# Block-compressed attention, window attention and a routed feed-forward in one kernel: narrower compressed scores, the mask as a VectorE addition, compression in two strips, and new orders of the work

## The reference

```
kb = k[:, :nb * CS].reshape(b, nb, CB, -1) + pe[None, None]
vb = v[:, :nb * CS].reshape(b, nb, CB, -1) + pe[None, None]
ck = jnp.einsum('bnkd,k->bnd', kb, wk_comp)
cv = jnp.einsum('bnkd,k->bnd', vb, wv_comp)
sc = jnp.einsum('bhsd,bhnd->bhsn', q4, ck4) * SCALE
comp_mask = (jnp.arange(nb) + 1) * CS <= jnp.arange(s)[:, None]
a_comp = _masked_softmax(sc, comp_mask[None, None])
out_comp = jnp.einsum('bhsn,bhnd->bhsd', a_comp, cv4)
imp = sc.mean(axis=(1, 2))
_, top_idx = jax.lax.top_k(imp, TOPK)
```

## Time and profile before

| | |
|---|---|
| median of 3 runs | 2564.87 us |
| the profiled execution | 2562.29 us |
| its span, first to last instruction | 2560.4 us |
| mean granted TensorE clock | 0.96 of full |
| busy: TensorE, VectorE, ScalarE, GpSimd | 88, 68, 57, 35% |
| instructions | 55188 |
| DMA | 90.10 MB, mean 35 GB/s |

### The profile page before, as it was taken

How to read it: one execution, slowest core, us unless ns; L and a number is a source line. 1 busy time by engine, 2 the same in 40 slices (tenths; PEclk the granted TensorE clock), 3 DMA queues, 4 the chain that set the end, 5 groups by cost and what they waited for, 6 DMA issues and landing times.

```text
span 2560.4 us, 55188 instructions
## 1 busy us (share of the span) xinstructions
PE 2241.7 (88%) x18184; PEld 1447.0 (57%) x18184; DVE 1747.1 (68%) x4612; ACT 1446.9 (57%) x4829; POOL 889.9 (35%) x780
## 2 busy tenths in 40 slices
PE   3888999899998999989998999989999899977676
PEld 0756666556664666556664666646665566644443
DVE  3466777578776777667786677757777578765654
ACT  1245666556654666556664566646665466645553
POOL 0435333333334333243332433343332433333221
PEclk9998999999998999989999999989999899998888
DMA  6010001100011000110002000110001100020000
GB/s 213 21 34 14 26 26 34 55 26 22 26 43 47 18 26 26 41 48 26 26 22 68 22 26 18 51 39 26 26 26 38 51 26 22 22 66 17 13 18 13
DMA packets 48844, 90.10 MB, mean 35 GB/s; under 512 B 6760, under 2 KB 6760, under 8 KB 48544
## 3 DMA queue, kind: packets, MB, share of 16 engines
q1 hardware_dynamic: 39328, 69.51, 8.9%
q10 hardware_dynamic: 9216, 16.78, 1.8%
HBM read 69.45 MB, written 16.83 MB: 34 GB/s over the span
## 4 chain that ended last, share of the span: by engine, by line
issue 56%; POOL 28%; PE 8%; ACT 3%; DVE 3%; DMA 1%; POOLq 1%; SPq 0%; DVEq 0%; ACTq 0%
POOL csp L1211 6%; POOL css L1203 4%; POOL xc L1238 3%; POOL h_lo L1231 3%; POOL ra L1243 3%; POOL kr L1195 3%; POOL ra L1195 3%; POOL wo_s L1219 1%; ACT pw L982 1%; PE ps_m L690 1%; POOL wbt_s L1225 1%; PE ps_o L622 1%; PE ps_m L495 1%; PE ps_m L497 1%; PE ps_m L496 1%
## 5 line engine op out<-in xcount | busy, mean ns | idle before, releaser
L982 ACT ACTIVATE pw<-ps_s,wmax 128x128 f32<-128x128 f32 x1024 | 358.6, 378 | 147.3 <-DVE wmax L1455 147.3
L495 PE MATMUL ps_m<-w_hi,h_hi 128*128 128x512 f32 x768 | 352.8, 459 | 75.6 <-DVE rbf L1422 31.5
L992 ACT ACTIVATE pw<-pw,wden 128x128 f32<-128x128 f32 x1024 | 313.2, 388 | 124.3 <-DVE wden L1465 124.3
L1015 ACT ACTIVATE pT<-ps_s 128x512 f32<-128x512 f32 x240 | 142.4, 593 | 306.2 <-PE ps_s L616 222.7
L497 PE MATMUL ps_m<-w_hi,h_lo 128*128 128x512 f32 x768 | 308.3, 401 | 0.0
L496 PE MATMUL ps_m<-w_lo,h_hi 128*128 128x512 f32 x768 | 307.7, 401 | 0.0
L690 PE MATMUL ps_m<-wbt_s,h2T 128*128 128x512 f32 x512 | 259.7, 613 | 0.4 <-ACT zs L998 0.4
L655 PE MATMUL ps_m<-wo_s,aT 128*128 128x512 f32 x512 | 252.5, 616 | 0.9 <-ACT aT L1019 0.8
L1231 POOL TENSOR_TENSOR h_lo<-hT,h_hi 128x512 fp32r<-128x512 f32 x57 | 72.2, 1267 | 514.1 <-ACT h_hi L933 514.1
L495 PEld LDWEIGHTS ps_m<-w_hi,h_hi 128*128 128x128 f32 x768 | 147.7, 192 | 176.6 <-issue 90.1
L1211 POOL TENSOR_TENSOR csp<-csp,cden 128x256 f32<-128x256 f32 (+1 forms) x128 | 169.7, 1345 | 221.4 <-DVE cden L1504 221.4
(11 more groups left out here) (189 smaller groups left out, 4614.0 us busy)
## 6 DMA issues: line engine op xcount, KB each, us to landing
xa<-x_in SPq DMA_DIRECT2D x65, 256.0 KB, 2.7
xc<-x_in SPq DMA_DIRECT2D x64, 256.0 KB, 2.7
out<-t ACTq DMA_DIRECT2D x64, 256.0 KB, 2.0
wo_s<-wo_in SPq DMA_DIRECT2D x8, 1024.0 KB, 6.1
wbt_s<-wbt_in SPq DMA_DIRECT2D x8, 1024.0 KB
gbc<-gate_rows SPq DMA_DIRECT2D x24, 256.0 KB, 5.2
pw<-wmod_in SPq DMA_DIRECT2D x3, 1024.0 KB, 5.6
pT<-wmod_in SPq DMA_DIRECT2D x3, 1024.0 KB, 5.2
```

Source lines behind the costliest of these rows:

```text
L495: pe_.matmul(ps[:], h_hi[:, c, :], w_hi[:, col, c, :], start=(c == 0), stop=False)
L982: ins = act.activation(pw[:, hw, :], ps_w[:, j, i, 1, :], ACT.Exp, bias=wmax[:, hw:hw + 1], accum_out=wden[:, 0, hw:hw + 1])
L992: act.activation(pw[:, hw, :], pw[:, hw, :], ACT.Copy, scale=wden[:, 2, hw:hw + 1]).then_inc(wn_ok, 1)
```

## The change

- The compression scores go only over the 16 selected columns and the first 8 (t + 1) blocks: `cs_scores`, `cs_max`, `cs_subtract`, `cs_exps`, `cs_factor`, `cs_normalise` have 16 + 8 (t + 1) columns, that is 24 to 80. `transpose_cs`, `probs_copy` and `cs_values` take 72 to 128 rows.
- The four mask products are gone. `csmask` is float32, and VectorE adds it while it evacuates the scores (`cs_mask`), in place of ScalarE's `cs_copy`.
- `compress` writes two strips of 32 partitions: strip k takes tiles 4k to 4k + 3. `pe` is padded with zeros to 128 rows, so that all its products have 128 rows.
- The end part has functions of its own (`end_first`, `end_slot`, `last`) with orders of their own.
- The orders of `first_slot`, `slot` and `turn` are new on all four engines, and so are the banks.
- `gather` waits for the copy of the last V; the prologue's `split_h` waits for Q, K and V of the tile before. Part A, the loads and their order on SP's queue, the stores, and the prologue's `head` are otherwise as before.

The diff, cut to its core (for TensorE and VectorE the new order of a slot; `a` and `c2` conditions left out):

```
+def blocks_seen(t):
+    return (t + 1) * (P // CB)
...
-        csmask = sb("csmask", [P, NT, CS], BF16)
+        csmask = sb("csmask", [P, NT, CS])
...
-        parts = ((0, NSEL), (NSEL, CS))
+        def parts(t):
+            return (0, NSEL), (NSEL, NSEL + blocks_seen(t))
...
             def compress(seg, b, ba, tiles):
-                dst = ps_cv[NB:P, :]
+                half, per = NT // 2, NB // 2
+                strip = [ps_cv[NB + per * k:NB + per * (k + 1), :] for k in range(2)]
...
+                    for k in range(2):
+                        pe_.matmul(strip[k], pew[:, 0:per], pe_s[:, :], start=True, stop=False, skip_group_check=True)
...
+                    for k in range(2):
+                        mm = pe_.matmul(strip[k], blkw[:, off:off + per], v_s[:, half * k + t, :], start=False,
+                                        stop=(t == half - 1), skip_group_check=True)
...
             def cs_scores(b, t):
-                for j in range(4):
-                    pe_.matmul(ps_s[:, j, 0:4 * CS].rearrange("p (c n) -> p c n", c=4), ident_b[:, :],
-                               csmask[:, t, :].unsqueeze(1).broadcast_to([P, 4, CS]),
-                               start=True, stop=False, skip_group_check=True)
+                n = NSEL + blocks_seen(t)
                 for c in range(NC):
                     for j in range(4):
-                        mm = pe_.matmul(ps_s[:, j, c * CS:(c + 1) * CS], qT[rows, c, t * P:(t + 1) * P], csk[rows, c, :],
-                                        start=False, stop=True, skip_group_check=True)
+                        mm = pe_.matmul(ps_s[:, j, c * CS:c * CS + n], qT[rows, c, t * P:(t + 1) * P], csk[rows, c, 0:n],
+                                        start=True, stop=True, skip_group_check=True)
...
-            def cs_copy(b, t):
...
+            def cs_mask(b, t):
+                T = NT * b + t
+                n = NSEL + blocks_seen(t)
+                dve.wait_ge(s_full, QUADS * b + quad(t, "cs") + 2)
+                dve.wait_ge(cs_exp, 2 * T + 1)
+                mask = csmask[:, t, 0:n].unsqueeze(1).unsqueeze(1).broadcast_to([P, 2, 4, n])
+                for p in range(2):
+                    ins = dve.tensor_tensor(css[:, 8 * p:8 * p + 8, 0:n].rearrange("p (j c) n -> p j c n", j=2),
+                                            ps_s[:, 2 * p:2 * p + 2, 0:4 * CS].rearrange("p j (c n) -> p j c n", c=4)[:, :, :, 0:n],
+                                            mask, ALU.add)
+                ins.then_inc(s_done, 1)
```

More of the change, by code:

```diff
@@ L106 @@
 SETUP_UNITS = [(f"MOD{i}", 0, i % 2) for i in range(6)] + [("MODT", 0, 0)]
[L108 to L112 removed]
+HEAD_UNITS = [("HT", 0, 2)] + [(u, t + (u == "HT"), bank) for t in range(NT - 1) for u, bank in HEAD_ORDER]
@@ L115, in m_unit @@
+TURN_UNITS = [(u, NT - 1, bank) for u, bank in TURN_ORDER if u not in C2_UNITS and u != "HT"]
+SEGMENTS = {"pro": SETUP_UNITS + HEAD_UNITS + TURN_UNITS,
+            "loop": units_of([FIRST_ORDER] + [SLOT_ORDER] * (NT - 2) + [TURN_ORDER]),
+            "epi": units_of([END_FIRST_ORDER] + [END_SLOT_ORDER] * (NT - 2) + [LAST_ORDER])}
 def m_unit(seg, b, name, t):
@@ L742, in first_slot @@
+                transpose_cs(b, 1, 2)
+                feed(seg, b, t, [2, 3])
+                transpose_window(b, 1, 2)
+                transpose_z(seg, b, t)
                 window_values(b, 1, 1)
                 cs_values(b, 1, 1)
+                project(seg, b, t, "V", 2, [0])
+                feed(seg, b, t, [NC])
+                transpose_cs(b, 1, 3)
                 transpose_window(b, 1, 3)
+                project(seg, b, t, "V", 2, [1])
                 window_values(b, 1, 2)
-                feed(seg, b, t, [1])
```

680 lines of the change are left out of this document (387 added, 293 removed).

## The result

The changed kernel takes 2414.09 us (median of 4 runs, 2411.82 to 2416.61) against 2563.86 us for the kernel before in the same session. The ratio is 0.9415, with a 95% interval of 0.9399 to 0.9432: faster, by 150 us. The forecast was 2397 us, with a range of 2340 to 2485. The profiled execution took 2411.8 us (span 2410.0), against 2562.3 (span 2560.4).

The account below looks back on a forecast made before the run. TensorE, 88% busy, was taken as the bound, except a chain of small steps in the last batch. Middle slots 80, turns 28, first slots 15 and last batch 45 sum to 168 us: 2562.3 - 168 + 2.6 = 2397 us, range 2340 to 2485.

Parts of the forecast that it names:

- only what is removed counts: Rival, whole kernel: each reordered wait comes back elsewhere, so 2506 us; chance 15 in 100.
- The mask products: Every tile: dropping four products saves 0.65 us of TensorE, which nothing hides in a middle slot.
- I cost this at nothing: VectorE in a slot: mask addition gains 1.3 us, narrower passes lose 0.8; about 27 of 32.5 us busy, no cost.
- Scores over fewer blocks: Compression scores in a middle slot: 20 of 80 columns fewer at 0.41 ns each save 0.13 us; bounds nothing and 0.27.
- narrow products cost as wide ones: Rival, compression scores: fewer columns save nothing, 12 us comes back, 2409 us; chance 8 in 100.
- The order of a middle slot: 42 middle slots: qT wait (0.69) goes, rotation wait (0.75) stays; new slot 32.5 us, 1.9 less, 80 us with removed work.
- bare the tail of the slot: Rival, middle slots: late normalisation and splits leave 5.3 us a slot open, 2667 us, slower; chance 5 in 100.
- Compression in two strips: Turn: strips overlap, five pairs take 4.65 us for 8.4, 3.7 less; with mask 28 us over eight turns, bounds 12 and 40.
- Not all of it reaches the end: Turn: scores come 3.5 us earlier, but the chain from K's rotation to gather, importance some 2.5 us earlier, limits the gain.
- The first slot: First slot of 7 batches: 2.2 us less each, 15 us, mostly less waiting for kT; bounds minus 2 and plus 5.
- The last batch: End orders gain 45 us: 5.7 for six slots, 7 first slot, 4 tail; bounds 10 and 65.
- the walk: Last batch: following one slot through with profiled durations gives 27 us for 34; such a walk forgets waits.

Follow-up runs that it names:

- the contents alone: Kernel before with narrower scores and passes, mask on VectorE and two strips, but all old orders and the old end part: 2483.7 us, ratio 0.9686.
- the late weights: Changed kernel with the 1 MB load of the feed-forward weights (wbt) issued only after the window scores of tile 1: 2398.53 us, ratio 0.9352.
- 2384 us: Changed kernel with late feed-forward weights, and the clamp of tiles 2 to 7 moved behind the first window maximum: 2383.76 us, ratio 0.9307.
- the run with the old beginning of the first slot: Kernel with late clamp and late feed weights, three places starting the first slot put back on ScalarE, VectorE and TensorE: 2414.15 us, ratio 0.9436.

## Why the prediction was right, and where not

The direction, the size and the mechanism of most of it were right; the time came out 17 us above the forecast. The rival that only what is removed counts (2506 us) is out: the orders give 70 us. By the forecast's own steps:

- **The mask products**: shown, but mis-sized. Back in the changed kernel they cost 29 us, not 42. "I cost this at nothing", of VectorE's addition, was the step that failed: it moved the clamp of 32 elements into GpSimd's split, in four of seven passes of tile 6 and in all of tile 7, for 1.0 us each time.
- **Scores over fewer blocks**: the 0.13 us a middle slot, 12 us in all for the scores, were nothing. The rival "narrow products cost as wide ones" was right on this term. The fixed part that both rows showed was nearly all of the 71 ns a product.
- **The order of a middle slot**: the wait for qT is gone and the one for the rotation stays, as said, at 0.45 to 0.65 us rather than 0.75. New slot forecast 32.5, measured 32.36 in tiles 2 to 5 and 33.45 in tile 6: 64.2 us for these 35, against 66.5 by the forecast's 1.9 each. That the normalisation would bare the tail of the slot did not happen; no wait for it is left. That the slot came out so close is in part luck: the mask is worth 0.47 us in it rather than 0.65 and the narrower scores nothing, yet the contents alone give 1.1 us a slot, where the two terms make 0.78.
- **Compression in two strips**: 0.95 us a pair, as forecast from the value products. The turn with tile 7 gains 6.56 us where 1.9 + 3.5 were forecast. "Not all of it reaches the end" was too careful: the run with one strip shows that it does, 4.3 us a turn for 3.4 us of work. But I counted eight turns, and the eighth, in the prologue, brought nothing: the prologue takes 1.0 us more.
- **The first slot**: the step that failed. "The jump stays", and 2.2 us a batch were to be gained; instead the slot lost 1.6 us a batch in six passes, 22 us away from the forecast with the first pass counted, which is more than the whole miss. What was left out is that an engine which arrives at the jump together with a megabyte of loads gets its next instructions late: 6.6 us in place of 3.9 in the mean on VectorE, which is 2.2 us of the two stretches. The order did not give what I had for it either. With the late weights the two stretches take 56.9 us, 0.6 less than before, and TensorE is busy 1.0 us less in them: it stands 12.5 us a pass, against 12.1 before. The waits for `h_lo` and kT have turned into the one for the exponentials. The whole old order with the same contents takes 56.5. I had read the jump on TensorE alone, where it was 3.09 us, and not on VectorE, where the earlier trace rows has none and its idle time before the same copy was 4.77 us.
- **The last batch**: 45 forecast, 47.7 measured; slots of 26.5 us in the mean where the walk gave 27. Taking off a part for forgotten waits was not needed there, but the first slot and tile 1 gave 3.1 us and not 7. The walk had no term for the clock, which is at its lower level for 34 us less.

What stays open: how the load of the weights lengthens the jump. The DMA engines are 71% busy between 1041 and 1048, and the page has queues of its own for instructions, q8 and q14. The two packets of q14 start later when the weights are under way, and VectorE starts 1.7 to 2.7 us behind them. That they carry VectorE's and ScalarE's next instructions, and stand behind the weights' packets, fits all passes, but is inferred from these times. Of the 3.9 us that remain without the weights, 1.4 to 1.6 pass before these packets start; why is not known. Nor is it known what 0.44 us of the middle slot's 1.1 in the run without orders is beside the mask products, or whether the old order of the first slot with the late load would be faster than 2384 us.

## What to carry to other kernels

Read a loop's jump on every engine, not on the one that bounds, and ask which loads are under way in those microseconds: moving a load away from it can be worth as much as an order. When work goes to another engine that "has room", look at what is queued behind it and at what the engine beside it does at that moment; an instruction of 0.2 us on the path can cost 1.3. A long wait on the bounding engine is not in itself a fault of the order: undo the order before blaming it, and read the granted clock of both runs. Two orders whose waits differ by 0.8 us differed by 4.2 us in how long TensorE was busy with the same instructions.

## What the runs showed of the hardware

- **Jump and loads.** VectorE's first instruction after the loop's jump came after 6.74 us beside a load of 1 MB, and after 3.9 us in the mean with that load later (39.5 and 23.3 us for six). Two packets of an instruction queue started 4.0 to 4.6 us behind the branch in the one, 1.4 to 1.6 us (once 2.5) in the other. The idle time need not stand right behind the branch: with the mask products back, VectorE had a copy 0.5 us behind it and stood after that copy (33.9 us for six).
- **Waits and clock.** In the run with the old beginning of the first slot, passes with TensorE at the 1.2 GHz level for 14, 21 and 27 us took 58.0, 60.9 and 64.0 to 64.4 us.
- **VectorE beside GpSimd.** A clamp of 128 x 32 float32 elements, read and written without PSUM, took 0.18 us alone and 1.30 us when GpSimd's pass over 128 x 512 began 0.01 us before it, 1.01 us when that began 0.29 us before it (tile 7); each time it ended within 0.06 us of GpSimd's. VectorE's passes with PSUM operands ran beside the same GpSimd passes at their usual length. The Trainium skill, "SBUF — State Buffer", section Who interferes with whom, says that a `tensor_scalar` on SBUF can run in a mode that takes the ports VectorE shares with GpSimd, and that the engine which issues first then holds them for its whole instruction. The rows agree, though no row shows which mode the clamp ran in.
- **Strips of rows and columns.** 16 products over strips of 32 rows took 1.09 us at 24 columns, 1.12 at 64 and 1.13 at 80; eight over strips of 32 rows took 1.15 at 256. Two products into column strips of 32 took 0.95 us, one after another into a strip of 64 took 1.8.
